# A DLRM tower kernel: norm products ahead of the projection, row-major late layers, last block in two halves

## The reference

```python
e = jnp.stack([tbl_0[ids[:, 0]], ..., tbl_25[ids[:, 25]]], axis=1)      # 512 x 26 x 64
x = layer_norm(dense_t @ Wd.T, gd, bd)                                  # 512 x 128
y = layer_norm(jnp.einsum('bnd,ed->bne', sparse_t, Ws), gs, bs)         # 26 rows of 128
y = jnp.einsum('bne,pn->bep', y, Wsi)                                   # mixed to 32
y = layer_norm(y, gsi, bsi)                                             # over the 32
T = jnp.concatenate([x[:, None, :], jnp.swapaxes(y, 1, 2)], axis=1)     # 33 rows of 128
Z = jnp.einsum('bnd,bmd->bnm', T, T)                                    # 33 x 33
out = layer_norm(Z[:, TRIL_I, TRIL_J] @ Wl.T, gl, bl)                   # 528 -> 512, first 384 used
h = jnp.concatenate([out[:, :384], r_dense_t], axis=1)
h = jnp.maximum(h @ W_top1 + b_top1, 0.0)                               # 640 -> 512
h = jnp.maximum(h @ W_top2 + b_top2, 0.0)                               # -> 256
y = h @ W_top3                                                          # -> 1
```

## Time and profile before

| | us |
|---|---|
| runs | 299.91, 303.85, 304.52 |
| median | 303.85 |
| span of the profiled execution, first to last instruction | 185.4 |
| median less span, what lies around it | 118.4 |
| TensorE / VectorE / ScalarE / GpSimd busy | 148.0 / 130.1 / 106.9 / 104.3 |
| mean granted clock of TensorE | 0.936 |

### The profile page before, as it was taken

How to read it: one execution, slowest core, us unless ns; L and a number is a source line. 1 busy time by engine, 2 the same in 40 slices (tenths; PEclk the granted TensorE clock), 3 DMA queues, 4 the chain that set the end, 5 groups by cost and what they waited for, 6 DMA issues and landing times.

```text
span 185.4 us, 4668 instructions
## 1 busy us (share of the span) xinstructions
PE 148.0 (80%) x1825; PEld 113.2 (61%) x1825; DVE 130.1 (70%) x300; ACT 106.9 (58%) x245; POOL 104.3 (56%) x111
## 2 busy tenths in 40 slices
PE   0089877977969947459996978899799799977995
PEld 0084544434549544419794947569596666877994
DVE  6269659772959594908697999579799967943142
ACT  1202435594868486866667877585877857831230
POOL 3778777877878777777777777777840000020000
PEclk9999999996999669855999999999999999997899
DMA  5816334141111112311111123111111100110000
GB/s 153 294 33 194 137 58 161 32 139 26 34 21 29 24 28 61 61 27 27 28 33 23 32 58 64 28 28 25 28 25 40 33 7 11 27 38 0 0 0 0
DMA packets 6003, 9.59 MB, mean 52 GB/s; under 512 B 2303, under 2 KB 3538, under 8 KB 5854
## 3 DMA queue, kind: packets, MB, share of 16 engines
q0 software_dynamic: 3392, 3.45, 10.3%
q1 hardware_dynamic: 2232, 5.08, 9.1%
q10 hardware_dynamic: 358, 0.78, 1.1%
HBM read 8.01 MB, written 0.00 MB: 43 GB/s over the span
## 4 chain that ended last, share of the span: by engine, by line
PE 40%; ACT 23%; DVE 19%; issue 11%; DMA 5%; ACTq 1%; DVEq 0%
PE psB L318 11%; ACT Zs L639 10%; DVE B L831 4%; ACT U L600 4%; DMA dense_sb<-in_dense 4%; PE psG L284 4%; DVE qA L809 4%; DVE prod L802 3%; PE psZ L333 3%; PE psW L352 3%; PE psU L299 3%; DVE ssB L838 3%; ACT sdB L617 2%; PE psB L520 2%; PE psZ L424 2%
## 5 line engine op out<-in xcount | busy, mean ns | idle before, releaser
L257 POOL DMA_INDIRECT g_sb<-in_table,row_id x104 | 102.8, 989 | 31.7 <-issue 31.4
L831 DVE TENSOR_TENSOR B<-psB,bias 128x512 f32<-128x512 f32 x31 | 20.0, 686 | 26.2 <-PE psB L318 26.2
L639 ACT ACTIVATE Zs<-psZ 32x264 f32<-32x264 f32 x59 | 36.3, 616 | 2.1 <-PE psZ L333 1.0
L318 PE MATMUL psB<-U,ws_g 64*128 64x512 f32 x64 | 20.9, 735 | 15.3 <-ACT U L600 15.2
L611 ACT ACTIVATE sqB<-B 128x512 f32<-128x512 f32 x31 | 19.1, 632 | 23.1 <-DVE B L831 23.1
L299 PE MATMUL psU<-wsi_x,g_sb 128*128 128x192 f32 (+4 forms) x128 | 23.3, 330 | 7.3 <-DVE g_sb L824 7.3
L299 PEld LDWEIGHTS psU<-wsi_x,g_sb 128*128 128x128 f32 x128 | 20.9, 206 | 11.1 <-DVE g_sb L824 11.0
L284 PEld LDWEIGHTS psG<-gram,sT 128*128 128x128 f32 x104 | 14.0, 207 | 14.5 <-ACT sT L587 10.0
L850 DVE TENSOR_TENSOR T<-B,rB 128x512 f32<-128x512 f32 x31 | 21.5, 692 | 1.1
L838 DVE TENSOR_REDUCE ssB<-sqB 128x16 f32<-128x512 f32 x32 | 21.7, 677 | 0.1
L284 PE MATMUL psG<-gram,sT 128*128 128x128 f32 x104 | 17.2, 308 | 0.7 <-ACT sT L587 0.7
(11 more groups left out here) (159 smaller groups left out, 226.7 us busy)
## 6 DMA issues: line engine op xcount, KB each, us to landing
g_sb<-in_table,row_id POOLq DMA_INDIRECT x104, 2.5
wl_sb<-in_wl SPq DMA_DIRECT2D x1, 1280.0 KB, 6.0
w_sb<-in_w SPq DMA_DIRECT2D x2, 512.0 KB, 5.4
w_sb<-in_w SPq DMA_DIRECT2D x1, 768.0 KB, 4.5
small_sb<-in_small SPq DMA_DIRECT2D x1, 615.5 KB, 4.1
dense_sb<-in_dense ACTq DMA_DIRECT2D x1, 512.0 KB, 7.3
Zt<-Zs SPq DMA_DIRECT2D x3, 80.0 KB
Zt<-Zs SPq DMA_DIRECT2D x3, 70.0 KB
```

Of the source, the lines that this page charges most:

```text
L257: pool.indirect_dma_start(g_sb[:, k, h * DSP:(h + 1) * DSP], None, table, bass.IndirectOffsetOnAxis(row_id[:, 2 * k + h:2 * k + h + 1], 0) ...
L318: pe.matmul(psB[h][:, :], ws_g[h * DSP:(h + 1) * DSP, :], U[h * DSP:(h + 1) * DSP, u % 2, :], start=not (last and h == 0), stop=True).then ...
L639: act.activation(to, product, ACT.Copy).then_inc(Z_kept, 1)
L831: dve.tensor_tensor(B[:, h, :].rearrange("p (s j) -> p s j", j=PROJ), psB[h][:, :].rearrange("p (s j) -> p s j", j=PROJ), bias[:, :].rearr ...
```

## The change

In each step, `norms(t + 1)` now stands right behind `mix(t)` on TensorE, ahead of `project(t)`, and `transposes(t + 2)` stands at the step's end, one step earlier than before. VectorE does `mult_a` and `sums_a` of unit t + 1 ahead of `add_b`. ScalarE does `deviation_a(t + 1)` ahead of the squares, and `rows_out(t + 2)` last.

The late layers have samples on the partitions: `linear` is 5 products of 512 columns with Zt as weights; `keep_zc` copies its result, `square_z` squares it with a running sum, `turn_z` transposes it, `keep_zT` copies that, `top1` is 3 products of 512 columns, `add_h1` one VectorE pass (the deviation is a scalar a partition, hd gets its bias in `dense_part` by a one-row product), `turn_h` 4 transposes, `relu_h`, `layer2` 4 products of 256 columns, `add_h2` two VectorE passes, the second with a running sum, and `finish_y` scales 128 numbers. `GROUPS` makes the last block two groups of 64 samples, whose products are split in two column halves on TensorE (`n in range(g)`), put together by `fold` and `fold_y`; the first is relayed after unit 13, the second after unit 15, by three relays on SP and four on GpSimd. The output leaves in five DMAs.

Ahead of the loop the dense parts go (they are in steps 4, 5, 9 and 13, `HD_STEPS`), and `transposes(1)` is added. The load of wl is issued after that of the dense features, and ScalarE sums wl there. `x1_ready` is given at the end of ScalarE's step 3, before in step 1; `bias_part` in TensorE's step 3, which waits for it, is 4 products of 512 columns, before 12 of one column.

```diff
+HD_STEPS = (4, 5, 9, 13)
+GROUPS = ((0, 1), (1, 1), (2, 1), (LAST, 2), (LAST, 2))
...
+                for jj in range(lo, hi):
+                    for n in range(g):
+                        mm = pe.matmul(psL[k][n * s:(n + 1) * s, 0:w], zt_of(k)[0:KL, jj, :], wl_g[0:KL, jj, n * w:(n + 1) * w],
+                                       start=(jj == 0), stop=(jj == CW - 1))
...
             def bias_part():
                 pe.wait_ge(d_w1, 16)
                 pe.wait_ge(x1_ready, 1)
-                for f in range(K1):
-                    for k in range(KZ):
-                        mm = pe.matmul(psH[:, f:f + 1], w1_sb[:, k, f * P:(f + 1) * P], bl_c[:, k:k + 1],
-                                       start=(k == 0), stop=(k == KZ - 1))
-                mm.then_inc(bz_done, 1)
+                for k in range(KZ):
+                    pe.matmul(psH[0:1, :], bl_c[:, k:k + 1], w1_sb[:, k, :], start=(k == 0), stop=False)
+                pe.matmul(psH[0:1, :], one_r[0:1, 0:1], bs_sb[0:1, E:], start=False, stop=True).then_inc(bz_done, 1)
...
             transposes(0)
             norms(0)
-            x_part()
-            dense_part(2)
+            transposes(1)
 
             def step(t):
                 b, j = (t - LINEAR) // BU, (t - LINEAR) % BU
-                late = 0 <= b < LAST
+                late_step = 0 <= b < LAST
                 mix(t)
-                if t + 1 < UNITS:
-                    transposes(t + 1)
-                project(t)
+                if t == UNITS - 2:
+                    linear(b, 0, 2)
                 if t + 1 < UNITS:
                     norms(t + 1)
-                if late and j == 1 and t < UNITS - 1:
-                    linear(b, EARLY[b], ALL)
+                if late_step and j == 1 and t < UNITS - 1:
+                    turn_z(b)
+                if late_step and j == 2:
+                    turn_h(b)
+                project(t)
+                if t + 1 == UNITS:
+                    turn_z(b)
                 if t:
                     inner(t - 1)
-                if t == UNITS - 1:
-                    linear(b, EARLY[b], ALL)
                 if t == 0:
-                    dense_part(3)
+                    x_part()
                 if t == 1:
+                    shift_part(0, 3)
+                if t == 2:
+                    shift_part(3, CW)
                     x_sum()
-                    shift_part(0, 2)
-                if t == 2:
-                    shift_part(2, CW)
                 if t == 3:
                     bias_part()
-                if late and j == 0:
-                    if b:
-                        output(b - 1)
-                    linear(b, 0, EARLY[b])
-                if late and j == 1 and t < UNITS - 1:
-                    variance(b)
-                if late and j == 2:
-                    layer1(b)
-                if late and j == 3:
+                if t in HD_STEPS:
+                    dense_part(HD_STEPS.index(t))
+                if late_step and j == 0:
+                    linear(b, 2 if t == UNITS - 2 else 0, CW)
+                if late_step and j == 1 and t < UNITS - 1:
+                    top1(b)
+                if late_step and j == 2:
                     layer2(b)
+                if t + 2 < UNITS:
+                    transposes(t + 2)
 
             for t in range(UNITS):
                 step(t)
+            top1(LAST - 1, 0, 2)
             inner(UNITS - 1)
-            variance(LAST - 1)
-            third_layer1()
-            third_layer2(0, 2)
-            last_block()
+            top1(LAST - 1, 2, KZ)
+            linear(LAST)
+            turn_h(LAST - 1)
+            turn_z(LAST)
+            layer2(LAST - 1)
+            fold(LAST)
+            top1(LAST)
+            linear(LAST + 1)
+            turn_h(LAST)
+            turn_z(LAST + 1)
+            layer2(LAST)
+            top1(LAST + 1)
+            fold(LAST + 1)
+            fold_y(LAST)
+            turn_h(LAST + 1)
+            layer2(LAST + 1)
+            fold_y(LAST + 1)
...
             rows_out(0)
-            act.wait_ge(x_tr, 1)
-            act.activation(xT[:, :], psB[0][:, :], ACT.Copy).then_inc(xT_ready, 1)
+            sum_wl(0, 2)
             deviation_a(0)
-            keep_hd(2)
+            rows_out(1)
+            sum_wl(2, CW)
 
             def step(t):
                 b, j = (t - LINEAR) // BU, (t - LINEAR) % BU
-                late = 0 <= b < LAST
-                if late and j == 0 and b:
-                    relu2(b - 1)
-                if late and j == 2:
-                    deviation_w(b)
+                late_step = 0 <= b < LAST
+                if late_step and j == 1:
+                    keep_zc(b)
+                    square_z(b)
                 keep_u(t)
+                if late_step and j == 1 and t < UNITS - 1:
+                    keep_zT(b)
+                if late_step and j == 2:
+                    relu_h(b)
+                if t - 1 in HD_STEPS:
+                    keep_hd(HD_STEPS.index(t - 1))
+                if t == 4:
+                    act.wait_ge(bz_done, 1)
+                    act.activation(bz[:, :], psH[0:1, :], ACT.Copy).then_inc(bz_ready, 1)
                 if t + 1 < UNITS:
-                    rows_out(t + 1)
-                else:
-                    third_squares(0)
-                if late and j == 3:
-                    relu1(b)
+                    deviation_a(t + 1)
                 squares_b(t, 0)
                 squares_b(t, 1)
+                if t == 0:
+                    act.wait_ge(x_tr, 1)
+                    act.activation(xT[:, :], psZ[:, :], ACT.Copy).then_inc(xT_ready, 1)
                 enter_x(t)
-                if t + 1 < UNITS:
-                    deviation_a(t + 1)
-                if late and j == 1 and t < UNITS - 1:
-                    squares_w(b)
                 if 0 < t < UNITS - 1:
                     keep_z(t - 1, 0)
                 deviation_b(t, 0)
                 if t == UNITS - 1:
-                    keep_z(t - 1, 0)
+                    keep_zT(b)
                     deviation_b(t, 1)
-                    third_squares(1)
-                    keep_z(t - 1, 1)
-                    keep_z(t - 1, 2)
+                    for gq in range(3):
+                        keep_z(t - 1, gq)
                 elif t:
                     keep_z(t - 1, 1)
                     keep_z(t - 1, 2)
@@ -735,63 +744,46 @@
                     keep_z(t - 1, 3)
                 else:
                     deviation_b(t, 1)
-                if t == 0:
-                    keep_hd(3)
+                if late_step and j == 1 and t < UNITS - 1:
+                    deviation_z(b)
...
+                if t + 2 < UNITS:
+                    rows_out(t + 2)
...
+                if late_step and j == 2:
+                    add_h1(b)
+                if late_step and j == 3:
+                    add_h2(b)
+                    finish_y(b)
...
+                if t + 1 < UNITS:
+                    mult_a(t + 1)
+                    sums_a(t + 1)
                 if t < UNITS - 1:
                     add_b(t, 0)
                 add_b(t, 1)
                 if t + 1 < UNITS:
-                    mult_a(t + 1)
-                    sums_a(t + 1)
-                if late and j == 0 and b:
-                    copy_y(b - 1)
-                sums_b(t, 0)
-                if t + 1 < UNITS:
                     recip_a(t + 1)
                     scale_a(t + 1)
```

759 lines of the change are left out of this document (343 added, 416 removed).

## The result

| | before | changed |
|---|---|---|
| runs, us | 299.91, 304.52, 303.85, 301.58 | 307.33, 307.52, 307.91, 307.70 |
| median | 302.72 | 307.61 |
| ratio | | 1.026, 95% interval 1.020 to 1.032 |
| span of the profiled execution | 185.4 | 305.5 (its own time: 307.33) |

What follows compares the result with a forecast made beforehand. Bound by a ring of waits through TensorE, ScalarE and VectorE. Z copied at 163.7, plus 15.5 for TensorE's list and 1.9 for output, gives span 181.1, 4.3 less: 303.85 - 4.3 = 299.6 us, range 294 to 308.

Steps and rivals of the forecast that it cites:

- 118.4 lies around the span, and I keep that.: Whole run: median 303.85 less profiled span 185.4 taken as time outside the span, unchanged by the edit.
- step-3 wait: TensorE's bias_part waits 5.6 us for x1_ready, then takes 5.05 at mixed clock; unit 4's root to unit 5's: 14.6.
- Five small DMAs, 1.9.: Kernel's end: the output, now five small DMAs, takes 1.9 us, against 1.6 before.
- The ring, 7.6 a step.: Loop: one cycle of waits through ScalarE, TensorE and VectorE, from root to root, takes 7.6 us, against 8.03.
- 8.25 and 0.5: Loop: a step with four slots takes 8.25 us; linear adds 0.5 each in steps 6 and 10.
- ScalarE pays whole durations: Rival, loop: entries cost full durations, + 5 over ten steps, + 1.8 with bias_part at half clock; about 306.4, chance 0.13.
- 8.03 to 7.6: Loop: the new order of work shortens a step from 8.03 to 7.6 us.
- R(4): R(u) is the start of ScalarE's root of unit u's norms; for unit 4 claimed 55.5, 54 to 58, before 57.19.
- Mix 0, 1, 2 then start at 23.8, 31.2, 39.0: First steps: TensorE's first three mixes, behind transposes that wait for gathers, start at these times in us, as before.
- Z copied R + 13.9: End: the last copies of Z end 13.9 us after the last unit's root, at 163.7.
- 15.5 for TensorE's list: End: TensorE's work after the last Z copies takes 14.75 plus 0.75 of hand-overs, 15.5 us.
- the halves side by side: End: the last group's two column halves run at once on TensorE, half-width products priced at 0.43 per 256 columns.

Runs made afterwards that it cites:

- e1: The kernel before, unchanged, run again: 302.47 us, ratio 0.994; its profiled execution took 302.46 with a span of 300.6.
- e5: The changed kernel with the last block's 128 results turned into one row and written in one DMA from one partition: 190.53 us, ratio 1.028 to the kernel before.
- e15: The changed kernel, unchanged, measured a third time: 197.12 us beside 186.52 for the kernel before, ratio 1.055.
- e7: The changed kernel with only the loop's order put back to the old one: 193.23 us, ratio 1.043 to the kernel before.
- e12: The changed kernel with row output, early x1_ready and early copy of U(15), in the loop's old order: 292.97 us, against 293.21 in the new order.
- e6: The changed kernel with ScalarE's two copies that give x1_ready moved behind the copy of U(3): 190.42 us, ratio 1.028 to the kernel before.

## Why the prediction was wrong

**"118.4 lies around the span, and I keep that."** False: 1.8 us do. The span of 185.4 fits an execution without the standstill, the 303.85 is of runs with it. By itself this did not turn the sign, since I only added a difference; but it hid that the first 149 us of the measured runs follow other rules. There the changed kernel is further on when the standstill ends: R(3) is at 157.80, against 164.29 in e1. (Its prologue has no dense parts, so fewer instructions to wait for; that this is the reason is not shown.) The step-3 wait takes this back (R(5): 182.18 and 182.23), the loop gives 2.9 (R(15): 264.59 and 267.53), and the end turns it into 4.9 more span: R(15) to the end is 40.9, against 33.1 in e1.

**"Five small DMAs, 1.9."** This is the step that failed most, and in the measured pair it turned the sign: without its 5.4 the two spans (305.5 and 300.6) would differ by - 0.5, still not the gain I forecast. Without the standstill it is 5.4 of a loss of 10.2, and 4.8 would be left. It is a term with the wrong row behind it: I took the output DMA of one partition for DMAs of 64 and 128 partitions with 4 bytes each. They take 6.8 and 7.5 to land, 7.3 from the last VectorE instruction to the end: 5.4 too little. e5 shows it. The Trainium skill ("DMA: Bandwidth & Descriptors", Specifications) states that below 512 bytes the transfer becomes a read-modify-write; the direction agrees, but no run here tells that mechanism from the mere number of pieces.

**The ring, 7.6 a step.** Right in what it holds (`rows_out` releases the norm products, L302), wrong in size: 7.95 for a plain step where I had 7.6, and 9.0 to 9.1 for the two steps with four slots and linear (R(7) to R(8), R(11) to R(12)) where I had 8.25 and 0.5. I priced each ScalarE entry by the start of the next. A copy of Z ahead of a root or of `rows_out` holds it for 0.63, not 0.42: 141.80 to 142.43 and 144.12 to 144.76 in the rows of e15. That is the rival "ScalarE pays whole durations", to which I gave 0.13; it gave + 5, and + 3.8 was measured for R(5) to R(15). Its total of 306.4 lies near 307.61 by luck, since it leaves out the output's 5.4. 0.9 of the 3.8 is a wait of another kind, in the last section. At the same clock, from R(9) to R(15), the new loop takes 50.49 where the old kernel took 48.17. From R(5) to R(9) it takes 33.0 where the old took 38.2. The clock (0.82 before, 1.00 now) is a part of this, but not all: in e1 the kernel before took 37.9 there at 0.91. Ahead of the copies of U(5) and U(6) ScalarE prepares wl and hd there; for U(6) the mix had ended at 78.64:

```profile
77.92 1.47 ACT L754 ACTIVATE wl_g<-wl_sb,wl_off,gg 128x512 f32<-128x512 f32 x2
79.49 0.77 ACT L759 ACTIVATE wl_g<-psW,m_off,small_sb 34x512 f32<-34x512 f32 x1
80.17 0.71 ACT L766 ACTIVATE hd<-hd,b_z 128x512 f32<-128x512 f32 x1
80.78 0.58 ACT L600 ACTIVATE U<-psU 128x512 f32<-128x512 f32 x1
```

The changed kernel scales wl in steps 1 to 3 instead (L687), in e15 the last part behind the copies for which `bias_part` waits, while TensorE runs it. How much is the clock's and how much this, no run separates.

**The order.** "8.03 to 7.6" is refuted by e7 and e12: it gains 0.5 and 0.7 us over ten steps, and nothing over the whole kernel.

**The wait in step 3.** Right in place and mechanism, 15.46 for 14.6. The products of bias_part took 5.9, where 5.05 was my mean of both levels of the clock: 4.88 for L472, against 2.73 in e6. I foresaw it and still forecast a gain, since I let the loop and the end pay for it.

**R(4)** came at 57.6, inside my 54 to 58 but 2.1 behind the 55.5 that I built on. "Mix 0, 1, 2 then start at 23.8, 31.2, 39.0" became 25.4, 32.9 and 41.4 in e15, with mix 0 waiting for its gather (e7). **Z copied R + 13.9** became 14.6 (16.4 in the listed run); the granted clock of that stretch was 0.88 (0.79 there). **15.5 for TensorE's list** became 17.2; the halves side by side hold: 20 passes of 256 columns take 2.38, 0.12 each, where a pass of 512 takes 0.4.

## What to carry to other kernels

Set a profile's span beside the time of the same execution before you build on it. If they differ by more than a few microseconds, a part of the run is missing from the picture, and it may be the largest.

Price a DMA by a row of the same shape, partitions and bytes a partition, above all the last one of a kernel, since nothing covers it. A result of one number a partition is cheaper turned into a row first (0.95 us of work for 5.8 won; 4.6 measured in all).

Where the ring goes once through an engine's whole list, moving the others' work ahead wins nothing: the wait only moves to another place of that list. Shorten the list. An entry moved a step earlier can meet a load that isn't there yet. And before you compare two orders, count from a mark that stands at the same place of a step in both.
